# One pair of PSUM banks for the first five feed-forward units, and new call lists, in a fused decoder layer

## The reference

```python
def _L0_attn_ref(x, Wq, Wk, Wv, Wo):            # 16 heads of 16
    q, k, v = ...                               # x @ Wq, x @ Wk, x @ Wv
    scores = jnp.einsum('bthd,bshd->bhts', q, k)
    scores = scores * jnp.tril(jnp.ones((T, T)))
    attn = jax.nn.softmax(scores / T ** 0.5, axis=-1)
    return jnp.einsum('bhts,bshd->bthd', attn, v).reshape(B, T, H * Dh) @ Wo

def _L0_xattn_ref(k, v, q, ssm_kernel, D, head_dim):   # 16 heads of 8
    kv = jnp.einsum('bhil,bhjl->bijhl', k_, v_)
    y = ...                                     # causal convolution of kv with ssm_kernel (by fft)
    out = y + kv * D[None, None, None, :, None]
    return jnp.einsum('bijhl,bhil->bjhl', out, q_)...

def _L0_ffn_ref(x, ...):                        # 256 -> 2048 -> 256, 4-bit weights with scales
    gate, up = xt @ Wg.T, xt @ Wu.T             # dequantised
    return (gelu_tanh(gate) * up) @ Wd.T

x = x + _L0_attn_ref(_layernorm(x), ...)
x = x + _L0_xattn_ref(ctx_2048, ctx_2048, _layernorm(x), ...)
x = x + _L0_ffn_ref(_layernorm(x), ...)
```

## Time and profile before

| | |
|---|---|
| median of 3 runs | 261.29 us (260.91 to 262.44) |
| the profiled execution, its time | 262.25 us |
| its span in the trace | 260.5 us |
| TensorE busy | 244.8 us, 94% of the span |
| GpSimd, VectorE, ScalarE busy | 158.8, 155.1, 129.0 us |
| chain that ended last | 79% TensorE |
| first feed-forward unit starts | 126.8 us |

### The profile page before, as it was taken

The page is one execution under the profiler, slowest core; times in us unless marked ns, Lnnn a source line. Parts: engine busy times, 40 slices in busy tenths (PEclk is TensorE's granted clock), DMA queues, the critical chain, the costliest instruction groups (busy, mean ns, idle before and its releaser), DMA issues.

```text
span 260.5 us, 5009 instructions
## 1 busy us (share of the span) xinstructions
PE 244.8 (94%) x1872; PEld 158.3 (61%) x1872; DVE 155.1 (60%) x256; ACT 129.0 (50%) x281; POOL 158.8 (61%) x196
## 2 busy tenths in 40 slices
PE   7999999999998899886999999999999999999993
PEld 7755765556665567564546677665665565565562
DVE  2888668785897889989346732625437182421124
ACT  2354665477775777765475445225243243423230
POOL 4268455886129899998998964274562835532230
PEclk9999999999999999999799999999999999999999
DMA  6996996940340003000003000003021000000004
GB/s 195 348 355 197 158 262 168 150 125 0 104 145 1 4 0 99 32 1 0 4 8 113 3 0 0 3 1 119 5 67 54 3 0 0 0 4 0 0 3 161
DMA packets 15104, 18.81 MB, mean 72 GB/s; under 512 B 1448, under 2 KB 12776, under 8 KB 15080
## 3 DMA queue, kind: packets, MB, share of 16 engines
q1 hardware_dynamic: 15080, 18.49, 26.2%
HBM read 15.21 MB, written 3.15 MB: 70 GB/s over the span
## 4 chain that ended last, share of the span: by engine, by line
PE 79%; DVE 8%; ACT 4%; POOL 3%; issue 3%; DMA 2%; SPq 0%; DVEq 0%; ACTq 0%; POOLq 0%
PE bank L1223 38%; PE bank L1389 16%; PE bank L1279 3%; PE bank L1281 3%; PE bank L1295 3%; PE bank L1277 2%; PE bank L1463 2%; DMA X<-in_x 2%; PE bank L1414 2%; ACT PT L615 2%; PE bank L1461 1%; PE bank L1416 1%; PE bank L1347 1%; DVE o_sb L985 1%; PE bank L1331 1%
## 5 line engine op out<-in xcount | busy, mean ns | idle before, releaser
L465 POOL TENSOR_TENSOR QK<-QK 128x512 f16<-128x512 f32 x31 | 35.9, 1160 | 53.4 <-ACT QK L644 53.4
L1028 DVE SCALAR_TENSOR_TENSOR QK<-bank,QK 128x512 f32<-128x512 f32 x32 | 22.1, 691 | 60.9 <-PE bank L1223 57.6
L654 ACT ACTIVATE QK<-bank 128x512 f32<-128x512 f32 x32 | 19.0, 596 | 59.9 <-PE bank L1223 59.8
L1223 PE MATMUL bank<-xTh,Wa 128*128 128x512 f16 x128 | 40.7, 382 | 0.0
L1223 PE MATMUL bank<-xTh,Wb 128*128 128x512 f16 x128 | 40.7, 379 | 0.0
L441 POOL TENSOR_TENSOR arena<-Ys,qx 128x640 f32<-128x640 f32 x16 | 26.7, 1671 | 3.5 <-ACT qx L706 3.5
L1223 PE MATMUL bank<-xTl,Wa 128*128 128x512 f16 x64 | 24.5, 383 | 0.0
L1223 PE MATMUL bank<-xTl,Wb 128*128 128x512 f16 x64 | 24.3, 379 | 0.0
L968 DVE TENSOR_REDUCE mx<-bank 128x8 f32<-128x1024 f32 x16 | 19.5, 1218 | 6.9 <-PE bank L1312 6.9
L1389 PE MATMUL bank<-Wa,QK 128*128 128x256 f16 x192 | 23.4, 273 | 0.0
L1389 PE MATMUL bank<-Wb,QK 128*128 128x256 f16 x192 | 23.3, 273 | 0.0
(11 more groups left out here) (145 smaller groups left out, 502.5 us busy)
## 6 DMA issues: line engine op xcount, KB each, us to landing
arena<-in_codes SPq DMA_DIRECT2D x6, 384.0 KB
arena<-in_ker SPq DMA_DIRECT2D x2, 1024.0 KB, 12.1
QK<-qk_scratch SPq DMA_DIRECT2D x8, 256.0 KB, 6.0
arena<-in_ctx SPq DMA_DIRECT2D x2, 768.0 KB, 8.4
qk_scratch<-Wa SPq DMA_DIRECT2D x12, 128.0 KB, 3.6
arena<-in_gu_scale SPq DMA_DIRECT2D x6, 256.0 KB
QK<-qk_scratch SPq DMA_DIRECT2D x8, 128.0 KB, 5.9
out<-XN SPq DMA_DIRECT2D x4, 256.0 KB, 2.4
```

Of the source, the lines that this page charges most:

```text
L465: g_.tensor_tensor(il[:, u % IR], val[:, u % VR], ih[:, u % IR], ALU.subtract).then_inc(s_il, 1)
L654: s_.activation(val[:, u % VR], bank[2 * (u % 2)][:, :], ACT.Gelu_apprx_tanh, scale=1.0 / W_GAIN).then_inc(s_gel, 1)
L1028: v_.scalar_tensor_tensor(out=val[:, u % VR], in0=bank[2 * (u % 2) + 1][:, :], scalar=UP_SCALE, in1=val[:, u % VR], op0=ALU.mult, op1=ALU. ...
L1223: ins = mmul(out, a(c), w(c), start=(n == 0), stop=(n == 3 * len(chunks) - 1))
```

## The change

Three pieces of code and the lists. Units 0 to 4 all use banks 0 and 1; from unit 5 on the pairs alternate as before. Unit 0 waits for 8 exponentials (batches 0 to 3) instead of 16; unit 5, the first to write banks 2 and 3, waits for all 16. Units 1 to 4 wait for the gelu and the product of the unit directly before. `gate_gelu` and `gate_up` read the bank by `pair(u)`. SyncE loads the codes of steps 2 and 3 one `max_rows` later. All other lines of the diff put the same calls into another order, on all four engines, from the convolutions to unit 7.

```diff
+        ALONE = 4
+
+        def pair(u):
+
+            return 2 * (u % 2) if u > ALONE else 0
+
...
             max_rows(2)
+            max_rows(3)
             early_codes(2)
-            max_rows(3)
+            max_rows(4)
             early_codes(3)
-            max_rows(4)
...
                 if u == 0:
-                    sc.wait_ge(s_s, 2 * B)
-                    sc.wait_ge(s_stt, 2 * B)
+                    sc.wait_ge(s_s, B)
+                    sc.wait_ge(s_stt, B)
...
-                s_.activation(val[:, u % VR], bank[2 * (u % 2)][:, :], ACT.Gelu_apprx_tanh,
+                s_.activation(val[:, u % VR], bank[pair(u)][:, :], ACT.Gelu_apprx_tanh,
...
-                v_.scalar_tensor_tensor(out=val[:, u % VR], in0=bank[2 * (u % 2) + 1][:, :], scalar=UP_SCALE,
+                v_.scalar_tensor_tensor(out=val[:, u % VR], in0=bank[pair(u) + 1][:, :], scalar=UP_SCALE,
...
                 if u == 0:
                     pe.wait_ge(s_max, 2 * B)
+                    pe.wait_ge(s_exp, B)
+                elif u == ALONE + 1:
                     pe.wait_ge(s_exp, 2 * B)
...
-                for w, (out, signal) in enumerate(((bank[2 * (u % 2)], s_g), (bank[2 * (u % 2) + 1], s_u))):
-                    if u >= 2:
+                for w, (out, signal) in enumerate(((bank[pair(u)], s_g), (bank[pair(u) + 1], s_u))):
+                    if 0 < u <= ALONE:
+                        pe.wait_ge(s_gel if w == 0 else s_act, u)
+                    elif u > ALONE + 1:
                         pe.wait_ge(s_gel if w == 0 else s_act, u - 1)
...
+            gate_and_up(0)
             turn_heads(7)
-            turn_ffn(2)
-            add_cross(3)
-            project_out(6)
...
```

More of the change, by code:

```diff
@@ L1147, in _ @@
+            normalise(6)
+            stats_ffn(2)
+            stats_cross(4)
+            sum_slots(3, 0)
+            sum_slots(3, 1)
+            stats_cross(5)
+            stats_cross(6)
+            stats_ffn(3)
+            decode_codes(3)
+            ffn_lo(2)
+            normalise(7)
+            ffn_lo(3)
+            sum_slots(4, 0)
+            w_lo(2)
             sum_slots(4, 1)
+            gate_up(0)
+            stats_ffn(4)
             stats_cross(7)
-            ffn_lo(3)
+            gate_up(1)
@@ L1527, in _ @@
-            row_scores(4, 0)
             attend(1, 1)
             attend(1, 2)
-            turn_max(3)
             attend(1, 3)
+            row_scores(4, 1)
+            turn_values(1)
             turn_heads(0)
             key_scores(2, 0)
+            row_scores(5, 0)
             project_out(0)
+            key_scores(2, 1)
+            turn_heads(1)
+            row_scores(5, 1)
+            project_out(1)
             attend(2, 0)
-            row_scores(4, 1)
-            turn_values(1)
@@ L1538, in _ @@
-            key_scores(2, 1)
-            row_scores(5, 0)
+            turn_max(4)
+            turn_query(0)
             attend(2, 1)
             key_scores(3, 0)
-            turn_heads(1)
             attend(2, 2)
             attend(2, 3)
-            turn_query(0)
+            row_scores(6, 0)
+            turn_max(5)
+            turn_values(2)
             key_scores(3, 1)
             attend(3, 0)
-            project_out(1)
-            turn_values(2)
             attend(3, 1)
-            turn_max(4)
@@ L1565, in _ @@
-            attend(4, 2)
-            attend(4, 3)
-            row_scores(7, 0)
-            turn_query(1)
-            turn_heads(3)
-            add_cross(0)
-            key_scores(5, 0)
-            row_scores(7, 1)
-            project_out(3)
-            key_scores(5, 1)
-            turn_query(2)
+            attend(4, 1)
+            row_scores(7, 0)
+            key_scores(5, 0)
+            add_cross(0)
+            key_scores(5, 1)
+            attend(4, 2)
+            turn_values(3)
@@ L1576, in _ @@
+            attend(4, 3)
             turn_max(6)
-            turn_values(4)
-            turn_max(7)
+            add_cross(1)
             attend(5, 0)
             attend(5, 1)
+            turn_heads(3)
             attend(5, 2)
-            add_cross(1)
+            row_scores(7, 1)
+            turn_query(2)
+            project_out(3)
+            turn_values(4)
+            key_scores(6, 0)
             turn_ffn(0)
             attend(5, 3)
-            key_scores(6, 0)
+            attend(6, 0)
@@ L1586, in _ @@
+            attend(6, 1)
+            turn_ffn(1)
+            key_scores(6, 1)
             turn_values(5)
+            turn_max(7)
+            attend(6, 2)
+            attend(6, 3)
             turn_heads(4)
-            key_scores(6, 1)
+            turn_query(3)
             project_out(4)
-            turn_query(3)
-            attend(6, 0)
+            turn_values(6)
             key_scores(7, 0)
-            attend(6, 1)
-            attend(6, 2)
             turn_heads(5)
-            attend(6, 3)
@@ L1597, in _ @@
-            attend(7, 0)
-            attend(7, 1)
-            turn_ffn(1)
             add_cross(2)
             key_scores(7, 1)
-            turn_values(6)
             project_out(5)
+            turn_heads(6)
+            attend(7, 0)
+            project_out(6)
+            add_cross(3)
+            attend(7, 1)
+            turn_ffn(2)
             turn_query(4)
```

378 lines of the change are left out of this document (180 added, 198 removed).

## The result

The changed kernel took 265.10 us in the median of 4 runs (264.05 to 265.29), the kernel before in the same session 261.52 us (260.91 to 262.44). The two medians lie 3.6 us apart (1.4%); the ratio estimated from the executions is 1.011, with a 95% interval of 1.0079 to 1.0142. So the change is slower by 1.1%, about 2.9 us, or by somewhat more if one goes by the medians. 262.3 us was forecast and 265.2 was the range's upper end. The sign of the sum was right, its size was not.

The account below looks back on a forecast made before the run. TensorE, busy 244.8 of 260.5 us, was taken as the bound, so only its idle time and clock count. Terms -0.3 - 0.7 + 0.7 + 1.65 = +1.35, shortened by 0.35 to +1.0: 262.3 us against the median, range 259.0 to 265.2.

Parts of the forecast that it names:

- (a): Units 0 to 4 on one bank pair: only the first gelu, with its table load, is bare; +0.4 us, from 0 to 1.3.
- (b): Unit 0 waiting for 8 instead of 16 exponentials: the wait itself gives nothing, only unit 0's move ahead of four calls does.
- (c): Convolution stretch: `turn_max(0)` gets more cover but a decode comes ahead of the maxima; -0.3 us, bounds -1.2 and +0.6.
- (d): Attention up to `add_cross(3)`: uncovered trips fall from about 6.4 to about 5.7 us; -0.7 us, bounds -1.5 and +1.0.
- (e): From `add_cross(3)` to unit 0: idle waits sum to 3.6 us where 2.89 stood before; +0.7 us.
- (f): From unit 0 to unit 8: new waits before `project_out(7)`, `turn_query(6)` and `add_cross(5)`, plus (a)'s 0.4; +1.65 us.
- (g): TensorE's clock: the same half-speed dip as before; 0, bounds -1.7 us (no dip) and +1.7 us (twice).
- The sum: All terms of the whole kernel: +1.35 us, shortened by 0.35 to +1.0 us.
- a fifteenth: Cut of 0.35 us on the 5.25 us of new waits in (e) and (f), since old-order trips came out too long.
- the signs named beforehand: Among others: 3 to 4 us idle before unit 0, 0.3 to 1.4 before `turn_query(6)`, 4 to 5 in attention, dip again.
- The slower rival: GpSimd's queue behind `conv_products(4)` delays `rstd_cross(6)`, so `turn_query(6)` waits the full 1.35 us: +3.7, about 265 us; chance 0.27.
- The rule of the Trainium skill: GpSimd shares SBUF interfaces with VectorE, so meetings cost; alone it put the sum about 1.1 us higher, 0.1 us was taken.

Follow-up runs that it names:

- banks_old_lists: The kernel before with its own lists and only the change's bank rule (units 0 to 4 in banks 0 and 1): 265.87 us.
- unit0_back: The changed kernel with 11 filler matmuls of constants in its tail waits, and unit 0 moved back behind `add_cross(4)`: 269.29 us.
- fill_new: The changed kernel with 11 filler matmuls of constants in the three long TensorE waits of its tail: 264.73 us, 1.0100 to before.
- lists_two_pairs: The changed kernel's new lists with the old bank rule, pairs in turn and unit 0 after all 16 exponentials: 265.16 us, 1.0109 to before.
- rstd6_first: The changed kernel with 11 filler matmuls, `rstd_cross(6)` directly behind `rstd_ffn(3)` on GpSimd and `ln_eps(1, 6)` earlier on ScalarE: 263.40 us.
- tail_moves: The changed kernel with `rstd_cross(6)` first, other queue reorderings, four more moves (such as `turn_heads(7)` ahead of unit 0) and 5 filler matmuls: 261.31 us.

## Why the prediction was off in size

- **(a) banks, 0.4:** right. 0.41 us before unit 1, and in two pairs of runs no price that intervals of 0.2% to 0.4% to each side can show. That it rests on ScalarE's list (banks_old_lists: waits of 0.84, 1.33 and 1.75 us) was said as a condition.
- **(b) lower wait, 0:** as said, the gain is unit 0's forward move: 4.6 us with the late queue, half-speed time included (unit0_back). The lower wait alone was not run.
- **(c), (d) -1.0:** idle time fell by 0.4 and 0.9 us, 1.3 together. Right, a little small.
- **(e) +0.7:** the places were right, 1.05, 0.72 and 1.06 us before `turn_query(4)`, `turn_values(7)` and unit 0, where 1.15, 0.9 and 1.1 were forecast, and 0.1 before `turn_query(5)` instead of 0.4. But each came out smaller: 2.94 us in all instead of 3.6, against 2.89 before. So this term was nearly 0.
- **(f) +1.65:** 1.38 us in the trace of the change, 0.63 up to unit 1 and 0.75 before `add_cross(5)` (0.5 forecast). That is near the number, and by luck: unit 0 ran at half speed over the wait that was the question. **The step that failed is `turn_query(6)`, "0.4 taken" of 0 to 1.35.** With unit 0 at full speed it is 2.14 us, above the upper end, for which no working was given. The chain was counted as 5.4 us behind `rstd_ffn(3)`; the four rows took 6.8, because one of them ran beside `w_lo(2)` (2.61 instead of 1.05). I charged the contention to the rstd of batch 3 alone. Moving `rstd_cross(6)` back took 1.3 us off unit 1's start.
- **(g) clock, 0:** the dip was twice as long, the upper bound of +1.7. But it cost nothing in this trace, being hidden behind that chain (fill_new), so (f) and (g) are one loss and can't be added as if they were two: take the dip away and the wait stands in its place.
- **The sum:** -1.3, 0, +1.4 and +1.7 make the +1.8 of the profiled pair, where +1.0 was forecast. Shortening 5.25 us by "a fifteenth" does not follow from trips that came out a quarter too long; in proportion (6.4 to 5.12) it would have been 1.05 us, and the forecast +0.3. Of the signs named beforehand, the idle time in attention (4.21), the dip and the steady part came as said; the idle time before unit 0 (2.94) and the wait before `turn_query(6)` (0.22, or 2.14 without the dip) fell outside what was named.
- **The slower rival** (265, a chance of 0.27) was the case that came, with its place (GpSimd behind `conv_products(4)`) and its condition: the rstd ended 4.3 us after unit 0 had begun, beyond the 2.6 named. Its cause had one more member, the collision. That its 265 us is also the time measured is in part luck: it gave the attention no gain and (e) 0.5 us more, neither of which came, and it had no term for the clock.
- **The rule of the Trainium skill** on SBUF interfaces shared by GpSimd and VectorE (GPSIMD Engine Reference, section 1, Specifications) deserved more than the 0.1 us it got. The traces agree with it in three more places, in each of which VectorE's row reads two operands in SBUF: 2.61, 1.57 and 1.28 us for rows of 1.05, 0.54 and 0.42 us. Not every meeting costs: beside VectorE's reductions GpSimd's rows kept their 0.54 and 1.01 us.

**What stays open:** first, 1.8 of the 3.6 us, by which the medians differ more than the profiled pair does. 0.7 us of it lies on before's side: its profiled execution has the dip, and 262.25 us is above the median. 1.05 us lies on the change's side, at 264.05 in the profile and 265.08 to 265.29 in the others. These have more clock on average (0.990 to 0.994, against 0.987), so it isn't the length of the dip. The trace of lists_two_pairs offers a reason: there the dip missed unit 0 and fell on the calls after the 2.14 us wait, where nothing hides it. That the change's slower executions do this was not seen. Second, the 2 us by which rstd6_first is still above dip-free executions of before. Its trace shows the small waits that hold them, five from 0.34 to 0.75 us behind unit 0's start, but no run takes these away without adding others.

## What to carry to other kernels

When a list is reordered, write down for every small result that another engine waits for (an rstd, row maxima) how much long work now stands ahead of it in its queue, and add the collisions with the other vector engine to that work, not only to the step moved. A block moved forward covers a trip only up to its own length: unit 0, 2.6 us long, left 2.14 us of the trip behind it bare. One pair of banks for five units was free in the lists in which the releasing engine takes the release first, and cost 1.7% in those in which it does not; test the resource and the lists apart, since each alone told another story here (+1.7% and +1.1%, together +1.1%). And where executions fall into two groups by the granted clock, compare within a group before giving a small difference a cause.

## What the runs showed of the hardware

A GpSimd row on 128x1 (L358) took 0.54 us as a rule and 1.57 at 74.87 us of the change, beside this row of VectorE; GpSimd's L450 took 1.01 and 2.61 (at 123.28 us). It works the other way too: VectorE's L991 took 1.28 us instead of 0.42 at 118.61 us of tail_moves, while GpSimd multiplied.

```profile
74.29 1.73 DVE L1016 SCALAR_TENSOR_TENSOR Wa<-w,Wa 128x1536 f16<-128x1536 f32 x1
```

In these meetings the row that had begun first, or at the same time on VectorE, kept its length and the other one paid. VectorE's L1016 kept 1.73 us here; GpSimd's L447, begun 0.6 us ahead of the L991 of 1.28 us, kept 1.58. At 121.47 us of the change L991 began first, kept its 0.42, and GpSimd's L447 took 1.81.

The clock is not told by the longest wait alone. It was at 1.2 GHz for 6.8 us in the change, from 119.6 us on, after waits of 1.05 and 0.72 us close together. In lists_two_pairs the same two waits, one of 1.50 us and one of 2.14 left it at 2.4 GHz up to 128.3 us, and then it fell for 3.4 us. In unit0_back it fell for 6.8 us within a wait of 4.86. With the same 2.14 us wait it did not fall in the trace of fill_new, where fillers had run before. Sixteen fillers in waits cost nothing: the kernel before with them takes 261.29 us, and 261.25 without them where it has no dip.
